# Moving the cuts of the next batch's input, and of the coarsest level's output, to later places in a hand-written order of work

## The reference

```
for lvl in range(4):                       # every 1st, 2nd, 4th, 8th token
    x = query[:, ::2**lvl, :]
    outs.append(mha(x, in_proj_w[lvl], in_proj_b[lvl], out_w[lvl], out_b[lvl]))   # 16 heads of 16
current = outs[-1]
for lvl in (2, 1, 0):
    current = upsample_linear(current, outs[lvl].shape[1])
    current = current @ up_w[lvl].T + up_b[lvl] + outs[lvl]
x = layernorm(query + current)
h = silu(tlin(x, w1, s1)) * tlin(x, w2, s2)          # 256 -> 1024
h = gelu(tlin(h, h1, s)); h = gelu(tlin(h, h2, s))    # 1024 -> 1024, twice
x = layernorm(x + tlin(h, w3, s3))                    # 1024 -> 256
```

## Time and profile before

| what | value |
|---|---|
| median of three runs | 4003.92 us |
| profiled execution, its span | 4005.5 us, 4003.7 us |
| mean granted TensorE clock | 0.950 |
| PE busy | 3642.2 us (91%) |
| DVE busy | 2552.1 us (64%) |
| ACT busy | 2595.1 us (65%) |
| POOL busy | 1051.4 us (26%) |

### The profile page before, as it was taken

How to read it: one execution, slowest core, us unless ns; L and a number is a source line. 1 busy time by engine, 2 the same in 40 slices (tenths; PEclk the granted TensorE clock), 3 DMA queues, 4 the chain that set the end, 5 groups by cost and what they waited for, 6 DMA issues and landing times. The chain is left out here.

```text
span 4003.7 us, 70655 instructions
## 1 busy us (share of the span) xinstructions
PE 3642.2 (91%) x20993; PEld 1954.6 (49%) x20993; DVE 2552.1 (64%) x4806; ACT 2595.1 (65%) x3273; POOL 1051.4 (26%) x1024
## 2 busy tenths in 40 slices
PE   5899889989989989989988988869999999999998
PEld 3333333333333323333333332258878787887887
DVE  5778978878878887887897898523333333333333
ACT  2779778868868868877877978734444344443443
POOL 2233434434444343343443342210000000000000
PEclk6989989989989989998998999979999999999999
DMA  4423423422332332333332344210000000000000
GB/s 138 156 70 98 123 77 91 118 81 86 105 95 87 105 107 79 103 95 93 89 117 72 99 123 135 75 51 12 12 12 13 21 11 12 12 11 13 21 11 11
DMA packets 231920, 284.40 MB, mean 71 GB/s; under 512 B 53524, under 2 KB 189908, under 8 KB 230384
## 3 DMA queue, kind: packets, MB, share of 16 engines
q1 hardware_dynamic: 222272, 270.54, 22.5%
q10 hardware_dynamic: 9216, 8.39, 0.6%
HBM read 166.63 MB, written 108.00 MB: 69 GB/s over the span
## 5 line engine op out<-in xcount | busy, mean ns | idle before, releaser
L982 ACT ACTIVATE a_probs<-a_p_s,a_unit_now 128x1024 f32<-128x1024 f32 x1360 | 1448.7, 1111 | 351.9 <-PE a_p_s L1300 345.3
L1086 DVE TENSOR_REDUCE a_part_max<-a_p_r 128x1 f32<-128x512 f32 x2048 | 1301.6, 676 | 270.9 <-PE a_p_r L1313 266.4
L1313 PE MATMUL a_p_r<-a_k_st,a_q_st 48*128 48x512 f16 (+2 forms) x2944 | 921.0, 383 | 209.5 <-DVE a_part_max L1086 126.2
L1313 PEld LDWEIGHTS a_p_r<-a_k_st,a_q_st 48*128 48x128 f16 x2944 | 229.1, 94 | 1239.6 <-DVE a_part_max L1086 871.3
L1642 PE MATMUL p_h<-f_h_hi,f_w_hi 128*128 128x512 f32 x2048 | 807.3, 394 | 24.0 <-issue 24.0
L1642 PE MATMUL p_h<-f_h_lo,f_w_hi 128*128 128x512 f32 x2048 | 803.2, 392 | 0.0
L1330 PE MATMUL a_p_o<-a_probs,a_v_aug 128*17 128x512 f32 (+2 forms) x5888 | 747.5, 588 | 3.5 <-ACT a_raw L992 2.8
L1300 PE MATMUL a_p_s<-a_q_st,a_k_st 50*128 50x512 f16 (+2 forms) x2944 | 694.9, 376 | 25.9 <-ACT a_probs L982 24.0
L1613 DVE TENSOR_TENSOR f_h_lo<-f_h_f,f_h_hi 128x512 fp32r<-128x512 f32 x256 | 177.1, 692 | 697.2 <-ACT f_h_hi L1539 697.2
L1537 ACT ACTIVATE f_h_f<-p_h,f_sc 128x512 f32<-128x512 f32 x256 | 176.6, 690 | 556.7 <-PE p_h L1642 556.6
L1086 DVE TENSOR_REDUCE a_row_max<-a_p_r 128x1 f32<-128x512 f32 (+2 forms) x672 | 427.2, 676 | 98.2 <-PE a_p_r L1313 95.9
(11 more groups left out here) (131 smaller groups left out, 4533.6 us busy)
## 6 DMA issues: line engine op xcount, KB each, us to landing
qk_scratch<-a_qk_room SPq DMA_DIRECT2D x288, 128.0 KB
a_w_lo<-wqkv_inner SPq DMA_DIRECT2D x30, 768.0 KB, 4.3
a_q_st<-qk_scratch SPq DMA_DIRECT2D x64, 192.0 KB, 3.7
a_k_st<-qk_scratch SPq DMA_DIRECT2D x64, 192.0 KB, 4.8
a_a_lo<-a_attn SPq DMA_DIRECT2D x384, 32.0 KB, 2.0
a_o_lo<-wo_inner SPq DMA_DIRECT2D x24, 512.0 KB, 3.7
a_qk_room<-wf SPq DMA_DIRECT2D x22, 512.0 KB, 3.8
w_lo_scratch<-a_qk_room SPq DMA_DIRECT2D x22, 512.0 KB, 2.7
```

The source lines that it names most:

```text
L982: act.activation(probs[:, s % 2, 2 * p:2 * p + 2, :], p_s[:, 2 * p:2 * p + 2, :], ACT.Exp, scale=unit_now[:, lvl:lvl + 1]).then_inc(exp_do ...
L1086: dve.reduce_max(out, src, AX.X).then_inc(max_read.sem, 1)
L1313: ins = pe.matmul(p_a[:, r * size:(r + 1) * size], q_st[rows_of(j, ROWS), query_at:query_at + 128], k_st[rows_of(j, ROWS), key_at:key_at + ...
```

## The change

Four numbers of `timeline` change for every batch but the first, and one for all.

- The places of xcut 0 and 1 go from 3 and 3.5 steps behind the load to 4.8 and 5.3.
- The place of the first wcut (level 2) goes from 4 to 4.8 steps behind the load, which is now the place of xcut 0.
- The spans of all four levels go 1.8 steps later, from 4.6 to 6.4 behind the load.
- The wanted places of the level 2 projections and values go 1.8 steps later, from 6 to 7.8 and from 7 to 8.8. By the rules above proj 0 and 1 come out 2 steps later and v 0 one step. The other levels follow: their weight loads come 1, 1 and 2 steps later, and their projections 0 to 2 and values 2 to 5 steps later.
- The acut of level 3 goes 1.2 steps later, from 6.4 to 7.6 steps behind the end of its unit.

```
-            side.update(places([(("proj", n), load_at[lvl] + 6 + gap[lvl] * i) for i, n in enumerate(mine)], taken, 2))
-            side.update(places([(("v", n), (6 if lvl == 0 else load_at[lvl] + 7) + (4 if lvl == 0 else 2) * kt) for n, kt in turns], taken))
+            side.update(places([(("proj", n), load_at[lvl] + (7.8 if lvl == 2 else 6) + gap[lvl] * i) for i, n in enumerate(mine)], taken, 2))
+            side.update(places([(("v", n), (6 if lvl == 0 else load_at[lvl] + (8.8 if lvl == 2 else 7)) + (4 if lvl == 0 else 2) * kt) for n, kt in turns], taken))
...
-    p += [(load_at[2] + 3 + (6 if first else .5) * n, "xcut", n) for n in range(2)]
+    p += [(load_at[2] + (3 + 6 * n if first else 4.8 + .5 * n), "xcut", n) for n in range(2)]
     for n, lvl in enumerate(W_ORDER):
-        cut_at = (load_at[lvl] + proj_at[lvl]) / 2 + 1
+        cut_at = (load_at[lvl] + proj_at[lvl]) / 2 + (1 if first or lvl != 2 else 1.8)
         p += [(load_at[lvl], "wload", n), (cut_at, "wcut", n)]
-        span_at = cut_at + .3 if first else load_at[2] + 4.6 + .4 * n
+        span_at = cut_at + .3 if first else load_at[2] + 6.4 + .4 * n
...
-    p += [(max(UNITS[u].end for u in cut.units) + 6.4, "acut", n) for n, cut in enumerate(CUTS)]
+    p += [(max(UNITS[u].end for u in cut.units) + (7.6 if cut.lvl == 3 else 6.4), "acut", n) for n, cut in enumerate(CUTS)]
```

## The result

The changed kernel takes 4013.82 us as a median (4008.22 to 4020.77), the kernel before 4006.41 beside it: ratio 1.0021, interval 1.0012 to 1.003. Measured a second time, with fewer runs, the ratio was 1.005 (1.0015 to 1.0085). So it is slower by 8 us or somewhat more, in the first measurement within the 0.3% that the prediction called no change. The forecast was 4021, with 3988 to 4042 as its range.

The account below looks back on a forecast made before the run. PE, DVE and ACT were taken to share the bound, with PE itself bounding the slow stretch. Six batches at +2.6 and the first at +1.4 gave 17.0 us on 4005.5: 4022.5, 4021 as a median, range 3988 to 4042.

Parts of the forecast that it names:

- X's cut no longer waits, the weight cut does, by 2.5 to 5 us: On ACT near x's load: x has landed, but ACT waits 2.5 to 5 us for the first weights before `a_w_hi`.
- PE is pinned 14.0 us behind the issue: PE resumes 14.0 us behind x's DMA issue instead of 6.8, set by the landing of the first weights.
- A wait of 1.7 us at the first span: PE waits 1.7 us (bounds 0 and 3) at the first span for `a_reach`, behind large cuts on POOL.
- 15.6 us of work at half clock to the common point, and 0.5 for the clock's tail: PE's work from resumption through proj 0 takes 15.6 us at half clock; low clock beyond it adds 0.5.
- The common point: Moment when proj 0 and score pair 69 are done, proj 1 not begun: 31.3 us behind x's issue, before 29.2.
- the clock comes back early: Rival, chance 0.17: full clock returns early in the stretch behind PE's resumption; sum -8 us, 3996 as a median.
- low clock for 17 to 21 us from the resumption: Sign expected in the changed profile: the low clock lasts 17 to 21 us from PE's resumption near x.
- Coarsest acut: 0: Moving the coarsest level's acut 1.2 steps later on ACT and POOL costs 0, gain and loss hidden by the stall.
- The moved proj, v and weight loads: 0, within 10: Later projections, values and weight loads, 1 to 5 steps later, cost 0, within -10 to +10 us.
- Rival: DVE decides: Chance 0.13: DVE bounds the slow stretch and saves 2.4 us a batch as `a_unit_qk` gets short; 4004 us.
- Rival: slower still: Chance 0.15: first-span wait over 1.7 us keeps the clock low beyond proj 0, 3 us a batch more; 4042 us.
- Rival: the stall really goes, 96 us: Chance 0.09: ACT reaches the weight cut after the weights land, so the stall near x goes; 96 us, 3908.

Follow-up runs that it names:

- The last run: Kernel with first weight cut at 32.55 and the earlier kernel's later places, second level's weight cut moved from 41.90 to 41.15: 3958.34 us, ratio 0.9886.
- the 2.6 version: Changed kernel with the first weight cut 0.8 steps later still (2.6 instead of 1.8), behind both x cuts: 3969.69 us, ratio 0.9917.

## Why the prediction came out as it did

The place of the new wait and its cause were right. That the sum then came out with the right sign was luck: it put 17 us on the stretch around x, which cost 0.1 to 0.6 us a body, and nothing on the later places, where the 8 us arose. The sum was too high by 9 us of 17, and its parts were wrong in both directions.

- *X's cut no longer waits, the weight cut does, by 2.5 to 5 us.* Right in kind, and a little small: 4.48 to 6.45 us in the six later bodies, over 5 in four of them, 0.86 in the first, none before the first `a_x_hi`.
- *PE is pinned 14.0 us behind the issue.* Right: 13.5 as a mean of the six (12.67 to 14.23), since `a_w_hi` came 9.1 us behind it instead of 9.55. In the repeated trace it was 9.8 and 14.2 us. That the order of the transfers sets it is shown by the run that swaps them.
- *A wait of 1.7 us at the first span.* It was 1.30 to 1.32 in all seven.
- *15.6 us of work at half clock to the common point, and 0.5 for the clock's tail.* This is the first step that failed, in size. From resumption to the end of proj 0 I had 17.3 us with the wait, plus 0.5; it was 15.8 as a mean of the six (in the second batch 14.76, above). In three to four bodies of seven the clock was back before proj 0, which then took 1.67 us instead of 2.93. I had put proj 0 at half clock in all because it was so before, although my own rival "the clock comes back early" named the other case. The common point lies 29.3 us behind the issue (30.0 in the repeated trace) instead of 31.3; before 29.2 (29.4 in its repeated trace). The predicted +2.1 to +2.6 a body was 0.1 to 0.6. The sign "low clock for 17 to 21 us from the resumption" failed with it: it lasted 11 to 13 us in four bodies and 17 to 20 in three.
- *Coarsest acut: 0.* Right as far as it can be told: 1.0007 (0.9998 to 1.0016), and at places 33 to 85 of a body 0.2 us or little more.
- *The moved proj, v and weight loads: 0, within 10.* The second step that failed. I looked for waits for the later weights' transfers, found none, and took 0. The price was on ACT's own queue: the second weight cut at 42.15 instead of 41.15 costs 1.05 us in each body, 7.4 in all, where the ratio gives 8.4 us (4.8 to 12.0). The last run shows it for 41.90 against 41.15; the changed kernel has the same 1.05 us between the same places in all seven bodies of both traces.
- *Rival: DVE decides.* `a_unit_qk` did become short, with a median of 197 ns instead of 1018:

```profile
L1110 DVE TENSOR_SCALAR a_unit_qk<-a_bound x32: 169/197/2866, 13.8 to 2148.9; 128x2 int32<-128x2 int32 x32
```

  The stretch gained nothing visible from it, so here it was no bound. With later spans 2.80 us of it stood ahead of maxima that PE waited for, in the second batch. The Trainium skill, "SBUF — State Buffer", section "Who interferes with whom", says that a DVE tensor_scalar in a two-port mode and a GpSimd instruction exclude each other for the whole instruction. The traces agree: 2.49 and 2.80 us where w_lo runs, ending with it, and 0.17 where it doesn't; which mode the instruction ran in no trace shows.
- *Rival: the clock comes back early.* True of proj 0 in four bodies of seven and in three of the repeated trace. Its sum, -8 us, was not reached, since the second weight cut added 7.4.
- *Rival: slower still.* The wait at the first span was 1.3 us and not over 1.7, and the low clock ended at most 5.7 us behind the start of proj 0, as before the change. The argument given for it, that a stretch with little work kept the clock low before, does not fit its own rows: PE was busy 16.24 of 16.50 us while the clock was low.
- *Rival: the stall really goes, 96 us.* Not in this kernel, but it can. With the weight cut behind x's it goes down to 1.4 us, and this gives 33 us, not 96. Half of the low clock stays (72 us). The prediction's 96 us took the whole slow stretch as won.

What stays open is why the low clock ended sooner with the changed order near x. PE had been idle as long or longer (7.1 to 8.0 us before in the six later bodies, 7.4 to 9.4 after), and the length of the low clock differs between bodies of one trace and between two traces of one program (130 and 144 us in sum).

## What to carry to other kernels

When a consumer is moved later than its data, look at what else stands between its new place and its start on the same in-order engine: here a cut whose data lands last had come ahead of it by a tie, and the wait was kept under another name. Order such cuts by the time at which their data lands, and then look at what waits for each of them: the same cut moved later still cost time again. And a task that shifts only because another pushes it is part of the change: look at which gap of the bounding engine it falls into, not only at whether its data is there.

## What the runs showed of the hardware

- The granted clock fell near x in every body of every version, also where PE's longest gap there was short. With gaps of 2.5 to 3.4 us (weights' transfer first) it was low for 17.1 us in all seven bodies; with gaps of 1.3 to 2.6 us (the 2.6 version) for 3.4 to 13.7 us. Later spans, with gaps of 1.4 to 2.3 us, had 13.7 to 20.5 us, so the length of the gap alone does not set it.
- Low clock near x and time go together only roughly. It was 72 us at ratio 0.9917, 102 at 0.9936, 120 at 0.9942 and 130 at 0.995, but also 82 at 0.9886, 85 at 0.9903 and 116 at 0.9965.
- It stays low while PE is busy. In the changed kernel with the weights first, PE was busy 15.21 of the 17.07 us:

```profile
539.63:556.70 17.07, 15.21 (x70) 5.49 (x70) 10.47 (x26) 8.80 (x10) 10.57 (x19) 0.50 0.06 14
```

- The landing of a transfer depends on its place in the order. With 1 MB of x ahead of them the weights (768 KB) landed 6.8 to 10.3 us behind their own issue, in both traces of the changed kernel; when they went first, 4.2 to 4.4 us behind it. X, then behind them, landed 3.9 to 5.1 us behind its issue, where it had been 3.6 to 4.4.
